# Causal attention on one core: units of four heads whose scores are made in groups of 32 rows, instead of units of two heads over 96 rows

## What is computed

```
scores = einsum('bhqd,bhkd->bhqk', q, k) / sqrt(16)
scores = where(causal, scores, lowest)      # a query sees itself and what is before it
attn   = softmax(scores)
out    = einsum('bhqk,bhkd->bhqd', attn, v)
out    = out.reshape(B, S, 192) @ w_out
```

## Time and profile before

| | |
|---|---|
| median of 3 executions | 1374.59 us (1372.58 to 1374.79) |
| span of the profiled execution | 1397.1 us |
| PE busy | 1113.2 us, 80% of the span |
| PE weight loads busy | 771.9 us, 55% |
| DVE busy | 586.6 us, 42% |
| ACT busy | 394.9 us, 28% |

### The profile page before, as it was taken

One profiled execution on the slowest core, in us unless ns is written; L12 is line 12 of the kernel. 1 busy time (PEld: TensorE's weight loads), 2 busy tenths in 40 slices (PEclk: granted clock), 3 DMA queues, 4 the chain that ended last, 5 costly groups with the idle time before them and its releaser, 6 DMA issues. The chain is left out here.

```text
span 1397.1 us, 24200 instructions
## 1 busy us (share of the span) xinstructions
PE 1113.2 (80%) x8646; PEld 771.9 (55%) x8647; DVE 586.6 (42%) x1737; ACT 394.9 (28%) x939; POOL 85.7 (6%) x128
## 2 busy tenths in 40 slices
PE   1999999998988889797793299955878978369992
PEld 0676677656565566555472177732645654247771
DVE  5272144224343465567486022215752672512222
ACT  2223312221414444343240133312421431013220
POOL 2000000000000000000000400022000000040003
PEclk9999988599999888898795599986979989579996
DMA  9100000000000000291003211118300000021113
GB/s 245 45 3 3 0 2 3 1 1 2 2 2 2 1 1 1 47 238 55 0 1 71 82 43 49 47 44 200 104 1 0 1 1 1 23 74 46 50 43 99
DMA packets 32137, 57.09 MB, mean 41 GB/s; under 512 B 3558, under 2 KB 28871, under 8 KB 31019
## 3 DMA queue, kind: packets, MB, share of 16 engines
q1 hardware_dynamic: 28856, 48.47, 12.8%
q0 software_dynamic: 3072, 6.30, 1.5%
q10 hardware_dynamic: 114, 1.04, 0.3%
HBM read 41.83 MB, written 13.86 MB: 40 GB/s over the span
## 5 line engine op out<-in xcount | busy, mean ns | idle before, releaser
L1932 PE MATMUL banks<-gu,sxT 96*128 x496 | 178.8, 505 | 0.8 <-ACT sxT L1967 0.4
L215 PE MATMUL banks<-xT,weights 96*96 96x512 f32 (+3 forms) x288 | 149.1, 668 | 1.2 <-ACT xT L616 0.9
L1333 ACT ACTIVATE work<-banks,nmax 128x128 f32<-128x128 f32 (+1 forms) x288 | 105.7, 418 | 108.0 <-DVE nmax L1372 107.7
L1993 DVE TENSOR_TENSOR h<-sg,banks 128x384 f32<-128x384 f32 x62 | 34.4, 555 | 237.7 <-ACT sg L1975 227.3
L1932 PEld LDWEIGHTS banks<-gu,sxT 96*128 96x128 f32 x496 | 93.1, 198 | 54.9 <-issue 8.1
L1372 DVE TENSOR_REDUCE nmax<-banks 128x2 f32<-128x256 f32 (+1 forms) x144 | 80.2, 557 | 64.7 <-PE banks L1277 62.4
L1252 PE MATMUL banks<-K,Q 96*128 96x128 f32 (+1 forms) x384 | 86.1, 351 | 11.1 <-PEq L88 11.1
L215 PEld LDWEIGHTS banks<-xT,weights 96*96 96x96 f32 (+3 forms) x288 | 53.5, 193 | 74.8 <-issue 67.3
L555 PE MATMUL banks<-Q,K 64*98 64x196 f32 (+2 forms) x960 | 78.7, 305 | 9.1 <-ACT work L688 9.1
L688 ACT ACTIVATE work<-banks 98x1024 f32<-98x1024 f32 (+1 forms) x48 | 49.2, 1025 | 114.7 <-PE banks L555 114.7
L555 PEld LDWEIGHTS banks<-Q,K 64*98 64x98 f32 (+1 forms) x960 | 67.2, 184 | 24.2 <-issue 22.5
(11 more groups left out here) (253 smaller groups left out, 1663.2 us busy)
## 6 DMA issues: line engine op xcount, KB each, us to landing
gu<-in_L2f_gu SPq DMA_DIRECT2D x1, 6912.0 KB, 36.7
xin<-slots_in SPq DMA_DIRECT2D x62, 96.0 KB, 1.9
slots_out<-y SPq DMA_DIRECT2D x62, 96.0 KB
gu<-in_L3f_gu SPq DMA_DIRECT2D x1, 5184.0 KB, 28.5
dn<-in_L2f_dn SPq DMA_DIRECT2D x1, 4608.0 KB, 47.6
slots_in<-zeros SPq DMA_DIRECT2D x1, 2976.0 KB, 22.5
dn<-in_L3f_dn SPq DMA_DIRECT2D x1, 2592.0 KB, 34.3
gu<-in_L2f_gu SPq DMA_DIRECT2D x1, 2304.0 KB, 13.1
```

The source lines that it names most:

```text
L215: ins = nc.tensor.matmul(out, lhs(k, rows), rhs(k, rows), start=(k == 0), stop=(k == 1))
L1333: ins = nc.scalar.activation(w.Pr[0:rows, s % 3, hh, 0:lay.width(t)], S(s)[0:rows, hh, 0:lay.width(t)], ACT.Exp, bias=w.nmax[0:rows, s % 4 ...
L1932: ins = nc.tensor.matmul(banks[:, 2 + 2 * par + n, 0:EF], w.sxT[:, par, k, :], w.gu[:, bass.ds(e, 1), k, n * EF:(n + 1) * EF].rearrange("p ...
```

## The change

`attend` is written anew for causal layers alone. A unit is now four heads of a tile; there are 12 units. The queries have four masked copies instead of 12: in each group of 32 rows lie two heads, one copy keeps the even heads and one the odd (`act_halves`, `dve_halves`), for two chunks. A score matmul takes 32 rows, at partition 0, 32 or 64, and the two PSUM banks of a unit are filled from two different groups of rows in turn. The mask goes first and opens the accumulation, and the scores are added to it. Scores have two sets of two banks, transposed weights two banks, of which a unit with t = 1 fills both ("halves", each with its own count in `turned` and `copied`), the output of a tile one bank. The lags between the steps become shorter in steps: pv of unit s-3, transposes of s-2, a finished tile after 3 to 7 steps. DVE takes a normalisation step after each of its larger instructions. `qT` and `rb` move into the work buffer, and in L2f 14 of 16 experts' first weights are loaded early instead of 12.

```diff
 PE:
-            for s in range(U + 10):
...
-                    if s >= 3:
-                        pe.wait_ge(exp_ready, s - 2)
-                    for hh in range(2):
...
-                            ins = nc.tensor.matmul(S(s)[r0:r0 + rn, hh, 0:lay.width(t)], lay.q(m, t, h, win),
-                                                   lay.k(m, t, h, win), start=(hh == 0 or kind != "causal"),
...
+            for s in range(N + 8):
...
+                    if s >= 2:
+                        pe.wait_ge(exp_ready, s - 1)
+                    for b in range(2):
+                        nc.tensor.matmul(S(s)[:, b, :, t * P:(t + 1) * P], env.ident16[:, :], env.mask16[:, :, :],
+                                         start=True, stop=False, skip_group_check=True)
+                    for e in range(2):
+                        for b in range(2):
+                            c, r = divmod(2 * k + b, 3)
+                            rows = slice(32 * r, 32 * r + 32)
+                            q0 = m * TOKENS + t * P
+                            ins = nc.tensor.matmul(S(s)[:, b, e, 0:(t + 1) * P], w.Q[rows, 2 * c + e, q0:q0 + P],
+                                                   w.K[rows, c, m * TOKENS:m * TOKENS + (t + 1) * P],
+                                                   start=False, stop=True, skip_group_check=True)
+                    ins.then_inc(scores_ready, 1)
+                u = s - 3
+                if 0 <= u < N:
+                    m, t, k = place(u)
+                    pe.wait_ge(copied, halves_before(u + 1))
...
+                u = s - 2
+                if 0 <= u < N:
+                    t = place(u)[1]
                     pe.wait_ge(exp_ready, u + 1)
+                    for half in range(halves(u)):
+                        if u >= 1 and half < halves(u - 1):
+                            pe.wait_ge(copied, halves_before(u - 1) + half + 1)
 DVE:
+                    nc.vector.tensor_reduce(w.nmax[:, s % 4, :].rearrange("p (b e) -> p b e", e=2), S(s)[:, :, :, 0:(t + 1) * P],
+                                            AX.X, ALU.max, negate=True).then_inc(max_ready, 1)
+                    between(1)
...
+                    for half in range(halves(u)):
+                        dve.wait_ge(turned, halves_before(u) + half + 1)
...
+                        nc.vector.tensor_copy(w.PT[:, u % 2, 2 * half:2 * half + 2, :, :].rearrange("p j c q -> p (j c q)"),
+                                              turned_bank(half)).then_inc(copied, 1)
+                        between(1)
...
+                between(2 if more_steps and s >= 6 else 1)
 causal_project:
-    act_heads = [(c, j) for c in range(2) for j in range(6) if (j >= 2 if rope else c == 0)]
+    act_halves = [(c, e) for c in range(2) for e in range(2) if rope or c == 0]
...
 buffers and loads:
+                    w.qT = w.work[0:CH, 0:2 * PN].rearrange("p (c n) -> p c n", c=2)
...
-    early = x.stored if x.shared else n - 4
+    x.early = early = x.stored if x.shared else n - 2
```

More of the change, by code:

```diff
@@ L1139, in _ @@
             dve.wait_ge(L1.added, 4)
[L1142 to L1198, removed]
@@ L1201, in attend @@
-def attend(nc, env, w, kind, ip, inner, into_x, behind_eps=None, behind_centre=False):
-    R, banks, ident = env.R, env.banks, env.ident
[L1208 to L1212, removed]
+UNITS = 3
+def attend(nc, env, w, ip, inner, into_x, behind_eps=None, more_steps=False):
+    R, banks, ident = env.R, env.banks, env.ident
+    tiles = [(m, t) for m in range(PAIR) for t in range(2)]
+    N = UNITS * len(tiles)
@@ L1218, in attend, with place @@
         projected, added, steps = sem("projected"), sem("added"), sem("steps")
[L1220 to L1225, removed]
+        def place(u):
+            tile, k = divmod(u, UNITS)
+            return (*tiles[tile], k)
         def S(u):
-            return banks[:, u % 3, :].rearrange("p (h k) -> p h k", h=2)
@@ L1230, in PTb, with halves, halves_before @@
[L1230 to L1235, removed]
-        OM = banks[:, 7, 0:3 * P].rearrange("p (h d) -> p h d", d=32)
+            return banks[:, 2 * (u % 2):2 * (u % 2) + 2, :].rearrange("p b (e k) -> p b e k", e=2)
+        def halves(u):
+            return 2 if place(u)[1] else 1
+        def halves_before(u):
+            return sum(halves(v) for v in range(u))
@@ new lines, in turned_bank, with tile_at, image_at @@
+        def turned_bank(half):
+            return banks[:, 4 + half, :]
+        O = banks[:, 6, 0:3 * P].rearrange("p (g q) -> p g q", q=P)
+        OM = banks[:, 7, 0:3 * P].rearrange("p (h d) -> p h d", d=32)
+        def tile_at(s, lag):
+            tile, k = divmod(s - lag, UNITS)
+            return tile if k == UNITS - 1 and 0 <= tile < len(tiles) else None
+        def image_at(s, lag):
+            tile = tile_at(s, lag)
+            return tile // 2 if tile is not None and tile % 2 == 1 else None
@@ L1363, in _, with between @@
             behind = None
-            both = kind == "causal" and behind_eps is not None
-            for s in range(U + 10):
-                if s < U:
-                    _, t, _ = units[s]
-                    rows = lay.rows(t)
+            def between(n):
+                for _ in range(n):
+                    if next(ahead, "done") == "done" and behind is not None:
+                        next(behind, None)
+            for s in range(N + 8):
+                if s < N:
+                    t = place(s)[1]
                     dve.wait_ge(scores_ready, s + 1)
```

193 lines of the change are left out of this document (72 added, 121 removed).

## The result

The changed kernel takes 1392.15 us (median of 5 runs, 1389.69 to 1401.5) against 1372.67 us for the kernel before on the same chip (1369.9 to 1374.79). The ratio is 1.0152, with a 95% interval of 1.0118 to 1.0186: slower by 19.5 us, where 1353 was forecast.

The account below looks back on a forecast made before the run. PE was taken to set the pace in mid-stage, a serial chain at the end. Body gain 8.2, end loss 4.1, charge 0.5: 3.6 us a stage, 21.6 for six; 1374.6 - 21.6 = 1353 us, range 1334 to 1389.

Parts of the forecast that it names:

- The scores: Attend's score matmuls: eight alternating 32-row passes overlap, taking 1.06 us with 256 columns, 0.63 with 128.
- Rival 4: Attend's scores: 32-row groups do not overlap, scores stay at 1.74 us, 1402 us in all; chance 0.04.
- Changing the shape: PE switching between full, 32-row and 32-column matmuls in each unit: 0.10 us for the entry into the scores.
- Rival 2: Each of 12 units: changing the tiling mode drains PE for 0.54 us instead of 0.10, 1373 us; chance 0.07.
- The steps: Four heads, t = 1, in attend: PE 2.85 us instead of 3.50, DVE 2.66, ACT 1.7.
- The ring: Attend's loop through PE and DVE: copies of one unit, pv, then the next unit's transposes, 2.62 us a unit.
- rival 1: Attend's steps: the ring does not overlap, steps wait 0.65 us or more on average, up to 1389 us; chance 0.13.
- The end: Attend stage from last scores ready to residual: 15.0 us instead of 10.9, losing 4.1 a stage.
- The body: First attend stage, first mask to last scores: 27.1 us instead of 35.3, gaining 8.2.
- I charge 0.5: Each attend stage: 0.5 us allowed for PE's waits and longer half clock at a beginning or end.
- Rival 3: Attend's body: small score matmuls drop the clock, 10 us at half clock costing 5 a stage, 1383 us; chance 0.06.
- The rest at nothing: Outside attend's stages: fewer masked copies, moved buffers and the experts' earlier loads change nothing, 0 us.

Follow-up runs that it names:

- e2: Changed kernel with every score product over all 96 rows instead of 32 (output not the reference's): 1385.3 us, ratio 1.0071.
- e3: Changed kernel plus ten 128-row products of zeros on PE right ahead of each attend stage: 1386.6 us, ratio 1.0073.
- e1: Kernel before, with each score product over only the 32 rows holding its head's queries, nothing else changed: 1560.2 us.
- e10: e8 plus one product of 128-row zeros for each bank of a stage's first three units: 1369.9 us, ratio 0.9969 to the kernel before.
- e4: Changed kernel with 96-row scores in each stage's first three units only (output not the reference's): 1365.5 us, ratio 0.9868.
- e12: Kernel before, unchanged, profiled a second time; its median is 1372.7 us.
- e5: Changed kernel plus four 128-row products of zeros in each of a stage's first three units: 1385.1 us, ratio 1.0044.
- e9: e5 with twice as many 128-row products of zeros, eight a unit: 1374.7 us, ratio 0.9996 to the kernel before.
- e6: e5 with the same number of products of zeros, but over 32 rows: 1406.0 us, ratio 1.0219 to the kernel before.
- e8: Changed kernel with the first 128 queries copied by GpSimd into zeros, so the first three units' scores use 96 rows: 1381.5 us, ratio 1.0038.

## Why the prediction was wrong, step by step

- **The scores, right.** Eight passes of 256 columns: 1.06 forecast, 1.06 measured (496.26 to 497.32), and 1.82 without the overlap (e2, forecast 1.74). With 128 columns 0.63 forecast, 0.65 measured in e3. Rival 4 (no overlap) fell.
- **Changing the shape, right.** Two masks and the entry take 0.31 us (495.95 to 496.26); ahead of 96-row scores two masks take 0.22 (e2, 510.19 to 510.41): 0.09 for the entry, 0.10 forecast. Rival 2 (the drain) fell: no unit shows half a microsecond.
  The Trainium skill, TensorEngine Tiling (Array Packing), Key Properties, has a change of tiling mode drain TensorE; what these rows show of that is 0.09 us going in and the 0.19 by which four 32-row passes of e1 (1.06) exceed four 96-row ones (0.87).
- **The steps, right at full clock.** DVE's maxima of two successive t = 1 units start 2.63 apart (2.66 forecast), and PE's scores 2.43 to 2.63 apart (2.45 to 2.7 forecast). The ring adds no more than that, so rival 1 fell as a cause. Waits matter in another way: at full clock more of them show. From after to e10 half clock falls by 107 us, and PE's busy time in the six bodies falls by 38.7 (210.1 to 171.4, with the added products of e10 in it), while its idle time in them grows from 4.5 to 11.0; so the bodies are shorter by 32 us, not by half of 107.

```profile
494.81 1.22 DVE L1309 TENSOR_REDUCE nmax<-banks 128x4 f32<-128x1024 f32 x1 [0.33 <-PE banks L1209]
...
497.44 1.22 DVE L1309 TENSOR_REDUCE nmax<-banks 128x4 f32<-128x1024 f32 x1
```

- **The end, right in kind and a little too small.** Forecast: 15.0 from the last scores, 4.1 lost a stage. In the first stage it is 14.2 (scores done at 499.75, residual at 513.98), a loss of 3.3; over all six 4.4 a stage. That 14.2 lies below the forecast is luck: the working had the projection at half clock, 2.93, and here it ran at full clock, 1.57 (last line below). With 2.93 it would be 15.6; in e10, whose projections take as long in sum as those of the kernel before, the ends lose 4.8 a stage. PE's timeline with its waits shows the queue of pv groups behind the last scores, each behind DVE's copies; the last line is the projection:

```profile
499.75 0.41 PE L1221 MATMUL banks<-work,V 128*17 128x128 f32 x8
...
505.82 0.63 PE L1221 MATMUL banks<-work,V 128*17 128x128 f32 x16 [0.62 <-DVE work L1327]
...
508.42 0.63 PE L1221 MATMUL banks<-work,V 128*17 128x128 f32 x16 [0.73 <-DVE work L1327]
...
511.82 1.57 PE L215 MATMUL banks<-weights,OT 96*128 96x192 f32 x8 [0.47 <-ACT OT L1288]
```

- **The body, wrong, and this is the step that failed.** 27.1 us forecast for the first stage, about 34 measured; a gain of 8.2 a stage forecast, 49 over six, and 6.3 to 7.8 measured. The working allowed for the kernel's old half clock at the beginning, and the term "I charge 0.5" stood for whatever the clock would do besides. That charge was the step that failed, mis-sized by ten times: half clock went from 25 to 29 us in the six bodies to 134, and with the clock brought back the same bodies are shorter by 5.4 us a stage (e10) to 6.1 (e4). When the rows are filled at the start (e4), the body comes out at 28.2 to 30.4, within 1 to 3 us of the working. Two of the prediction's own signs of being wrong were there, a body over 31 us and a clock of 0.50 inside it. That 1392 lies only 3 us above the stated range speaks for nothing: its upper edge came from the ring, which took no part.
- **Rival 3 was the mechanism, and the argument against it was the mistake.** It named rows 11: PE at 9.80 of 10 us busy on 64-row products, at half clock all the while. Against them I set that PE kept full clock through the middle of the old stage. That row belongs to 96-row products and says nothing about 32-row ones; e1 puts those into the very same place and the clock is gone. A better argument against it stood in the same trace, and would have misled as well: in L1, which has the 64-row scores of the earlier trace rows, the clock is 1.00 for 160 us (rows below, columns as in rows 1). And the half clock of rows 11 goes on through 6.4 us of the next projection (267.00 to 273.40), products of 96 and 97 rows. So narrow products had been seen at both levels and wide ones at the lower, and rows 11 were a warning, not a forecast. The place was off as well: I thought of a clock that falls in the middle, and it is one that doesn't rise at the beginning. The rival's 10 us a stage became 18 more than before (105 / 6), its 1383 became 1392, and its chance of 0.06 was too small for something of which the trace already showed a case.

```profile
267.00:273.40 6.40, 6.40 (x8) 1.91 (x6) 0.00 (x0) 1.23 (x2) 0.00 (x0) 0.50 0.00 0
297.30:457.60 160.30, 137.72 (x1471) 91.54 (x1469) 59.93 (x124) 47.00 (x70) 1.22 (x3) 1.00 0.01 2
```

- **The rest at nothing, right as far as can be told.** From the first stage on, 634.2 us against 631.9 in e12, and the kernel before itself has 641.4 in its first profile.
- **The comparison with the median.** I took the profile's 22.5 us over the median to be independent of the change. e12 shows that nearly all of it was: of 26.2 us between the two profiles 15.3 lie ahead of the first stage, 9.5 in the rest and 1.4 in the bodies.
- **A slip in a sum.** Waits of 3 us a stage either way are 18 in all, 1335 to 1371 about 1353, not 1336 to 1366. Nothing else hangs on it.

## What to carry to other kernels

Before you narrow a matmul to fewer rows for the sake of overlap, look for the places in the trace where narrow products already run, and read the granted clock in all of them; a busy PE at 0.50 is a warning that no row of the wide form answers. Where the rows disagree, as here, the cheapest test is the old kernel with the new rows and nothing else (e1): one expression, and it showed the loss without the rewriting. Price a clock term by the stretches it could cover, not by a round half microsecond, above all where a stage starts cold. And when a rewrite makes units larger, weigh the longer end against the body first: here even the cured bodies (38.5 us gained) left some 6 us after the ends.

## What the runs showed of the hardware that was not expected

- PE busy without a gap for 70.72 us stayed at half clock when two thirds of the score rows were left out, with the same instructions, order and waits that had full clock over 96 rows. The 64 rows that e1 leaves out hold nothing but zeros of the masked queries, and products of zeros over 128 rows brought the clock back within 3 to 6 us in three stages of six, and at twice the dose in all six, where the same number over 32 rows left it at half for 20 to 27 us in each (e5, e9, e6).
- Once the clock was up, the 32-row units of the changed kernel kept it to the end of the body (e4, e8 to e10); the opening units with t = 0, which have waits of 1 us among them, did not (e3). What in the mix of a later unit makes the difference was not tried.
- Two kernels near the edge (e5, e8) had stages of both kinds from the same program: 30.0 and 38.0 us in one execution of e5, and 30.6 and 36.9 for the fifth stage in e8's two profiles. Such a kernel's median says little about any one of its executions.
